# Attention by two key tiles: eight scores in runs of 3, 3 and 2, value products behind each run

## The reference

```python
x = x + 0.5 * ffn(layernorm(x), ...)
x = x + attn(layernorm(x), ...)
x = x + 0.5 * ffn(layernorm(x), ...)

# attn: 16 heads of 16 features; q, k, v and the output are linear with a LoRA update
scores = einsum('bhqd,bhkd->bhqk', q, k) * 16 ** -0.5
out = einsum('bhqk,bhkd->bhqd', softmax(scores), v)
# ffn: silu(x @ gate) * (x @ up) @ down, plus 8 of 512 experts picked by two top-8 of 64 keys
```

## Time and profile before

| what | us |
|---|---|
| median of 3 runs | 845.81 (844.18 to 845.85) |
| the profiled execution: its own time | 844.09 |
| the profiled execution: span, first to last instruction | 842.2 |
| PE busy / DVE busy / ACT busy / POOL busy | 807.8 / 681.3 / 473.4 / 188.5 |
| one attention group, groups 1 to 7 | 20.97 |
| groups 9 to 12, each about | 23.4 |

### The profile page before, as it was taken

The page is one execution under the profiler, slowest core; times in us unless marked ns, Lnnn a source line. Parts: engine busy times, 40 slices in busy tenths (PEclk is TensorE's granted clock), DMA queues, the critical chain, the costliest instruction groups (busy, mean ns, idle before and its releaser), DMA issues.

```text
span 842.2 us, 14291 instructions
## 1 busy us (share of the span) xinstructions
PE 807.8 (96%) x5424; PEld 517.7 (61%) x5424; DVE 681.3 (81%) x1116; ACT 473.4 (56%) x898; POOL 188.5 (22%) x202
## 2 busy tenths in 40 slices
PE   4799999999999999999999999999999999999996
PEld 4687888887876433333333434443458787888885
DVE  5898778787689999999999888889837877976854
ACT  3444333333342788888888888888963343333422
POOL 2441202011111033333332322133430202020200
PEclk9999999999999999999999999999999999999998
DMA  8010000000040242223333222300100000000000
GB/s 274 26 43 10 0 1 1 1 1 1 1 80 9 40 77 53 40 39 64 64 64 63 40 39 39 64 27 26 27 1 1 1 2 26 0 26 1 2 25 26
DMA packets 19300, 27.86 MB, mean 33 GB/s; under 512 B 4576, under 2 KB 13600, under 8 KB 19232
## 3 DMA queue, kind: packets, MB, share of 16 engines
q1 hardware_dynamic: 19040, 26.56, 14.3%
q10 hardware_dynamic: 192, 0.39, 0.2%
HBM read 12.09 MB, written 2.10 MB: 17 GB/s over the span
## 4 chain that ended last, share of the span: by engine, by line
PE 85%; DVE 7%; ACT 4%; issue 2%; DMA 1%; POOL 0%; SPq 0%; DVEq 0%; ACTq 0%
PE front_ps L1608 16%; PE front_ps L1589 13%; PE max_ps L1549 6%; PE ffn_gate_ps L48 5%; PE ffn_out_ps L731 5%; PE ffn_gate_ps L50 5%; PE ffn_gate_ps L49 5%; PE ffn_out_ps L733 5%; PE ffn_out_ps L732 5%; PE ffn_up_ps L50 3%; PE ffn_up_ps L48 3%; PE ffn_up_ps L49 3%; ACT probs L1739 2%; PE ffn_mix_ps L711 2%; DVE norm_xn L139 1%
## 5 line engine op out<-in xcount | busy, mean ns | idle before, releaser
L1819 DVE TENSOR_REDUCE maxima<-max_ps 128x2 f32<-128x1024 f32 x256 | 311.1, 1223 | 29.4 <-PE max_ps L1549 26.9
L1739 ACT ACTIVATE probs<-front_ps 128x512 f32<-128x512 f32 x512 | 277.5, 597 | 39.0 <-PE front_ps L1589 29.3
L847 ACT ACTIVATE ffn_tanh<-ffn_gate_ps 128x512 f32<-128x512 f32 x96 | 57.5, 599 | 222.2 <-PE ffn_gate_ps L50 222.2
L1608 PE MATMUL front_ps<-probs,values 128*32 128x256 f32 x2048 | 163.4, 391 | 4.5 <-ACT mixed_t L1744 4.1
L1080 DVE SCALAR_TENSOR_TENSOR ffn_gated<-ffn_tanh,ffn_gate_ps 128x512 f32<-128x512 f32 x96 | 65.7, 684 | 65.2 <-ACT ffn_tanh L847 65.2
L1608 PEld LDWEIGHTS front_ps<-probs,values 128*32 128x32 f32 x2048 | 40.8, 107 | 95.4 <-issue 55.4
L1589 PE MATMUL front_ps<-q_stack,k_stack 49*128 49x512 f32 x256 | 94.6, 446 | 0.0
L1549 PE MATMUL max_ps<-ffn_xlo,ffn_xhi 48*128 48x512 f32 x256 | 93.7, 447 | 0.0
L1589 PE MATMUL front_ps<-ffn_xhi,ffn_xlo 49*128 49x512 f32 x256 | 91.5, 455 | 0.0
L1489 POOL TENSOR_TENSOR inverse_sum<-turned,minus_one 128x16 f32<-128x16 f32 x15 | 43.7, 2913 | 207.4 <-ACT turned L1751 207.4
L1549 PE MATMUL max_ps<-k_stack,q_stack 48*128 48x512 f32 x256 | 88.0, 455 | 0.6 <-DVE maxima L1819 0.4
(11 more groups left out here) (204 smaller groups left out, 1288.6 us busy)
## 6 DMA issues: line engine op xcount, KB each, us to landing
q_stack<-block SPq DMA_DIRECT2D x48, 64.0 KB, 2.3
ffn_xhi<-block SPq DMA_DIRECT2D x48, 64.0 KB, 2.3
ffn_xlo<-block SPq DMA_DIRECT2D x48, 64.0 KB, 2.3
k_stack<-block SPq DMA_DIRECT2D x42, 64.0 KB, 2.3
x_sb<-in_x SPq DMA_DIRECT2D x4, 512.0 KB, 7.4
out<-x_sb SPq DMA_DIRECT2D x4, 512.0 KB, 2.9
ffn_out_rows<-in_down SPq DMA_DIRECT2D x4, 256.0 KB, 4.8
weights_again<-in_gate SPq DMA_DIRECT2D x2, 512.0 KB, 3.5
```

Source lines behind the costliest of these rows:

```text
L1608: mm = pe.matmul(mixed_ps[strip:strip + STRIP, at:at + HALF // 2], values[g % SLOTS][:, kt, j, :], probs[:, (g * KEY_TILES + kt) % PROBS, ...
L1739: act.activation(probs[:, tile % PROBS, j, half * HALF:(half + 1) * HALF], score_ps[:, n % RING, :], ACT.Exp, scale=SCORE_SCALE).then_inc( ...
L1819: v.reduce_max(maxima[:, g % 2, m // 2, m % 2, :], max_ps[:, m % 2, :, :], axis=AXIS_X).then_inc(pair_max, 1)
```

## The change

- **Two key tiles at a time.** Eight scores and four pairs of two key tiles are put on PE as runs of 3, 3 and 2 scores (`two_key_tiles`). Run A: score, pair, score, score, and only head 1 of the next pair. Then the first half of the mix of the key tile before. Run B: head 0 of that pair, score, score, pair, score; then the second half of that mix. Run C: score, pair, score; then both halves of the mix of the first of the two key tiles. `max_scores` and `ahead` take the heads that they are to do.
- **Single steps.** They stand between run B's mix and run C (`between`, which has the same cases as the loop before): rows at two = 0, `turn_out` at 1, `turn_group_max` at 2, update and product at 3. ACT does six exponentials, then these copies (`copy_mixed` first, at two = 0), then two exponentials. `turn_later` and `rows_later` of group 15 stand before run A, before run B's leading half pair, or behind run B's mix, by a count of runs.
- **Pairs ahead:** 7 in place of 6 (`EARLY`); 5 before the main loop in place of 4. The first two key tiles of group 0 have their own order (`first_two`).
- **Probabilities** have three places in place of two (`PROBS`).
- **Weights again:** the space is halved. The four wide pieces go through the whole of it, one at a time; the late ones still alternate between halves.
- **Used columns:** `copy_turned` and the last group's copy read 17 of each 32 columns (272 in place of 512 elements a row).

```diff
@@ -221,18 +221,15 @@
         self.fetch(sp, dram, piece, self.raw[piece]).then_inc(self.raw_in[piece], 16)
 
     def raw_again(self, i, places):
-        place = places[:, i % 2, :]
-        if self.AGAIN[i].startswith("late"):
-            return place[:, 0:CHUNK]
-        return place.rearrange("p (k f) -> p k f", k=KT)
+        return places[:, i % 2, :] if self.AGAIN[i].startswith("late") else places[:, :, :]
 
     def wait_again(self, pe, piece):
 
         pe.wait_ge(self.again_lo, self.AGAIN.index(piece) + 1)
 
     def load_again(self, sp, dram, i, places):
-        if i >= 2:
-            sp.wait_ge(self.again_lo, i - 1)
+        if i:
+            sp.wait_ge(self.again_lo, i if i <= 4 else max(i - 1, 4))
         self.fetch(sp, dram, self.AGAIN[i], self.raw_again(i, places)).then_inc(self.again_in[i % 2], 16)
 
     def split_again(self, pool, i, places):
...
+STRIP = 32
+
+
+def used_columns(bank):
+
+    return bank.rearrange("p (s x) -> p s x", x=STRIP)[:, :, 0:HD + 1]
+
...
-        act.activation(self.rows.rearrange("p t a b -> p (t a b)"), bank, ACT.Copy).then_inc(self.copied, 1)
+        act.activation(self.rows.rearrange("p t a b -> p (t a) b"), used_columns(bank), ACT.Copy
+                       ).then_inc(self.copied, 1)
...
-    EARLY, EARLY_IN_FRONT = 6, 4
-    RING, PROBS = 3, 2
-    OUT_TURN_AT, MAX_TURN_AT = 2, 6
-    COPY_AFTER = 3
-    UPDATE_AT, TURN_ROWS_AT, PRODUCT_AT = 5, 3, 5
+    EARLY, EARLY_IN_FRONT = 7, 5
+    RING, PROBS = 3, 3
+    TWOS = KEY_TILES // 2
+    TURN_ROWS_AT, OUT_TURN_AT, MAX_TURN_AT, PRODUCT_AT = range(TWOS)
+    UPDATE_AT = PRODUCT_AT
...
-    LATER_TURNS, LATER_ROWS = (1, 2, 3, 4), (3, 4, 5, 6)
+    LATER_TURNS, LATER_ROWS = (2, 3, 5, 6), (5, 6, 8, 9)
...
-        again = sb("weights_again", [P, 2, KT * HALF_INTER], F32)
+        again = sb("weights_again", [P, KT, HALF_INTER], F32)
...
-        turned = sb("turned", [P, 2, KEY_TILES // 2, 4, STRIP], F32)
+        turned = sb("turned", [P, 2, KEY_TILES // 2, 4, HD + 1], F32)
...
-            def max_scores(g, m):
-                if m == 0:
+            def max_scores(g, m, heads=(1, 0)):
+                if g >= GROUPS:
+                    return
+                if m == 0 and 1 in heads:
                     pe.wait_ge(stacks_in[g % SLOTS], (g // SLOTS + 1) * STACK_DMAS * 16)
-                if g * PAIRS + m >= 2:
+                if g * PAIRS + m >= 2 and 1 in heads:
                     pe.wait_ge(pair_max, g * PAIRS + m - 1)
-                max_pair(g, m, 1)
-                max_pair(g, m, 0).then_inc(pair_scored, 1)
+                for j in heads:
+                    scored = max_pair(g, m, j)
+                    if j == 0:
+                        scored.then_inc(pair_scored, 1)
...
-            def ahead(g, step):
+            def ahead(g, step, heads=(1, 0)):
 
                 later, m = divmod(step + EARLY, PAIRS)
-                if g + 1 + later < GROUPS:
-                    max_scores(g + 1 + later, m)
+                max_scores(g + 1 + later, m, heads)
...
+            def first_two():
+
+                early = iter(range(EARLY_IN_FRONT, EARLY + 4))
+                score(0, 0)
+                max_scores(1, next(early))
+                score(0, 1)
+                score(0, 2)
+                max_scores(1, next(early))
+                value_rows(TILES - 2)
+                max_scores(1, next(early))
+                score(0, 3)
+                score(0, 4)
+                max_scores(1, next(early))
+                score(0, 5)
+                value_rows(TILES - 1)
+                max_scores(1, next(early))
+                score(0, 6)
+                max_scores(1, next(early))
+                score(0, 7)
+                mix(0, 0, 0)
+                mix(0, 0, 1)
+
+            def run_later(run):
+
+                if run in LATER_TURNS:
+                    turn_later(LATER_TURNS.index(run))
+                if run in LATER_ROWS:
+                    rows_later(LATER_ROWS.index(run))
+
...
+            def two_key_tiles(g, two):
+                i, step, last_group = 8 * two, 4 * two, g == GROUPS - 1
+                tile = g * KEY_TILES + 2 * two
+                if last_group:
+                    run_later(3 * two)
+                score(g, i)
+                ahead(g, step)
+                score(g, i + 1)
+                score(g, i + 2)
+                ahead(g, step + 1, (1,))
+                mix(*divmod(tile - 1, KEY_TILES), 0)
+                if last_group:
+                    run_later(3 * two + 1)
+                ahead(g, step + 1, (0,))
+                score(g, i + 3)
+                score(g, i + 4)
+                ahead(g, step + 2)
+                score(g, i + 5)
+                mix(*divmod(tile - 1, KEY_TILES), 1)
+                if last_group:
+                    run_later(3 * two + 2)
+                between(g, two)
+                score(g, i + 6)
+                ahead(g, step + 3)
+                score(g, i + 7)
+                mix(g, 2 * two, 0)
+                mix(g, 2 * two, 1)
 
...
-                value_rows(10 + m)
+                if m < 4:
+                    value_rows(10 + m)
+            first_two()
             for g in range(GROUPS):
-                for kt in range(KEY_TILES):
...
-                    score(g, 4 * kt)
-                    ahead(g, 2 * kt)
-                    score(g, 4 * kt + 1)
-                    mix(*divmod(g * KEY_TILES + kt - 1, KEY_TILES), 0)
-                    score(g, 4 * kt + 2)
-                    ahead(g, 2 * kt + 1)
-                    score(g, 4 * kt + 3)
-                    mix(*divmod(g * KEY_TILES + kt - 1, KEY_TILES), 1)
+                for two in range(1 if g == 0 else 0, TWOS):
+                    two_key_tiles(g, two)
...
-                act.activation(turned[:, g % 2, :, :, :].rearrange("p t a b -> p (t a b)"), score_ps[:, n % RING, :],
-                               ACT.Copy).then_inc(ring_out, 1)
+                act.activation(turned[:, g % 2, :, :, :].rearrange("p t a b -> p (t a) b"),
+                               used_columns(score_ps[:, n % RING, :]), ACT.Copy).then_inc(ring_out, 1)
...
-                for kt in range(KEY_TILES):
-                    if kt == OUT_TURN_AT and g:
+                for two in range(TWOS):
+                    for i in range(8 * two, 8 * two + 6):
+                        exponential(g, i)
+                    if two == 0 and g:
+                        copy_mixed(g - 1)
+                    elif two == 0:
+                        value_rows(7)
+                    if two == OUT_TURN_AT and g:
                         copy_turned(g - 1)
-                    if kt == MAX_TURN_AT and g < GROUPS - 1:
+                    if two == MAX_TURN_AT and g < GROUPS - 1:
...
-                    for i in range(4 * kt, 4 * kt + 4):
+                    for i in range(8 * two + 6, 8 * two + 8):
                         exponential(g, i)
-                        if i == COPY_AFTER and g:
-                            copy_mixed(g - 1)
-                        elif i == COPY_AFTER:
-                            value_rows(7)
             copy_mixed(GROUPS - 1)
 
```

62 lines of the change are left out of this document (25 added, 37 removed).

## The result

The changed kernel takes 848.24 us (median of 7 runs, 847.57 to 850.56); the kernel before, run beside it, 844.70 (7 runs, 843.90 to 845.85). The ratio is 1.0047, with a 95% interval of 1.0037 to 1.0057: slower by 3.5 us. The forecast was 847.9 and a change of +2.2. The time came nearer to it than the change did, and that is luck: it was built on a median of 845.81 for the kernel before, which more runs put 1.1 us lower, and this error and the one in the change cancelled. Between the profiled executions the difference is 847.76 - 844.09 = 3.67 us.

A forecast was written before the change was run, and what follows sets the result against it. PE was taken to lead, with DVE close behind. Terms 2.4 - 1.3 + 0.1 + 1.0 + 0 summed to +2.2 us, forecast as 847.9 from the median 845.81; the case's own range was 845.5 to 851, the whole range 838 to 853.

The forecast's parts named there:

- Run B loses 0.32: Run B's mix starts at 2.69 us, not 2.37, held by a reduction; two key tiles take 4.93, not 4.61.
- reduction a: DVE's reduction of run A's whole pair, which frees the bank for run B's whole pair at 2.04 us.
- The price of a change of kind: On PE, fewer switches between scores and mixes cut two key tiles from 4.96 to 4.61 us, 0.35 less.
- The split pair: Pair b's head 1 waits for reduction d, its head 0 follows a mix; two key tiles without a step take 5.1 us.
- DVE's close: DVE's closing of the maxima at two = 2: costs 0.13 us with POOL idle, 0.52 in place of 0.19 with POOL busy.
- Groups without pairs: From the middle of group 14, two key tiles take 0.17 us more than 4.48, six times: +1.0 us.
- The step that failed: In group 0, one pair moves ahead, one change of kind goes, DVE's 16 reductions stay: 0, from -0.7 to +0.7 us.
- The line on stack loads: Single place for weights: stack loads of four groups later wait anyway; nothing to several tenths if a load slips.
- At nothing: Third place of probabilities, narrower copy and single place for weights were put at no gain in the sum.
- the waits of run B are not there: Rival: run B's reduction and exponential waits are absent; -10 us, 836; chance 0.30 together with the rival of all 22 us.
- DVE's cycle is longer: Rival: reductions take 1.22 us instead of 1.14 and POOL is busy at every close; +4.5, 852 us; chance 0.20.
- all of the 22 us arrive: Rival: the whole saving from fewer switches on PE shows, giving 823 us; chance 0.02.

The follow-up runs named there:

- e1: The changed kernel with DVE's reduction of a pair reading only 256 of each head's 512 columns; 845.57 us, ratio 1.0008 to the kernel before.
- e3: The changed kernel with reductions and exponentials both cut to 256 of 512 columns; 830.09 us, ratio 0.9825 to the kernel before.
- e4: The kernel before with reductions and exponentials both cut to 256 of 512 columns; 844.03 us, ratio 0.9999.
- e5: The changed kernel with PE's last two value rows placed before the first score of group 0; 849.50 us, ratio 1.0059 to the kernel before.
- e11: The changed kernel with 6 pairs ahead and 4 before the main loop, as before the change; 848.77 us, ratio 1.0051 to the kernel before.
- e8: The kernel before with only the side edits: third place of probabilities, narrower copies, one place for weights; 844.60 us, ratio 1.0000.
- e2: The changed kernel with each exponential doing only 256 of its 512 columns; 848.41 us, ratio 1.0045 to the kernel before.

## Why the prediction was right, and where its size was wrong

**The bound and the mechanism.** "Run B loses 0.32" was said to come from a reduction first and an exponential right behind it. All three figures for run B's mix, counted from run A's start, were met: 2.69 with both waits (2.70 to 2.72 measured, in all four places of a group), 2.65 with the exponential alone (e1: 2.65), 2.37 with neither (e3: 2.38). The bare length of two key tiles was put at 4.61 and is 4.62 in e3. Counted from run B's own start, the mix comes 1.23 to 1.24 us later at two = 1 and 2 (1.22 was forecast) and 1.09 to 1.12 at two = 3 and 0, where run B itself starts late. The price of a change of kind, 0.35 us for two of them, holds: the twins e3 and e4 differ by 1.39 = 4 x 0.35 in a group. The Trainium skill (TensorEngine Tiling (Array Packing), Key Properties: a change of tiling mode drains TensorE) names that mechanism. The twins agree with it in that fewer changes take less time; that the drain is what is paid, and not another cost of the change, no run separates. The kernel after shows that the rule alone, which would have given about 823 us, says nothing about what the waits leave.

**The split pair.** The order b, c, d, then head 1, and head 0 behind a mix, is what the trace shows, and the 5.1 for two key tiles without slack is 5.09. Three details differ. DVE stands idle twice in two key tiles, not once. Head 1 delays run A's mix by 0.14, not 0.17; and that delay doesn't carry over into run B, whose mix is fixed by reduction a. It is carried by DVE to run C's pair, 0.15 late. The sum comes out the same.

**By terms**, forecast and measured (the lengths are from run A to run A):

| term | forecast | measured |
|---|---|---|
| `two` = 0, 1, 2, 3 | 5.4, 5.5, 5.27, 5.1 | 5.37, 5.54, 5.20, 5.09 |
| groups 1 to 7 and 13, each | +0.3 | +0.20 to +0.24 |
| groups 1 to 7 and 13, together | +2.4 | +1.74 |
| group 8 | +0.1 | -0.07 |
| groups 9 to 12, each | -0.3 | -0.31 |
| groups 9 to 12, together | -1.3 | -1.21 |
| groups 14 and 15 | +1.0 | +0.89 |
| group 0 | 0 (-0.7 to +0.7) | +2.25 |
| sum | +2.2 | +3.6 |

The lengths are from 386.44, 391.81, 397.35, 402.55 and 407.64 in the kernel after. DVE's close was priced at the busy and idle POOL between them and took 0.33 to 0.34 us, so `two` = 2 is 0.07 shorter than I took. Without group 0 the terms came to +1.35 in place of +2.2; the miss in group 0 hid part of that. And 845.81 + 2.2 is 848.0, not 847.9.

**Groups without pairs.** Two key tiles of group 14 (run A, run B, its mix, the next run A):

```profile
601.75 0.73 PE L1602 MATMUL front_ps<-ffn_xhi,ffn_xlo 49*128 49x512 f32 x3
...
603.00 1.47 PE L1602 MATMUL front_ps<-ffn_xhi,ffn_xlo 49*128 49x512 f32 x3
604.39 0.64 PE L1621 MATMUL front_ps<-probs,values 128*32 128x256 f32 x8
...
606.39 0.74 PE L1602 MATMUL front_ps<-ffn_xhi,ffn_xlo 49*128 49x512 f32 x3
```

Run B at +1.25, its mix at +2.64, run C at +3.21, its mixes at +3.64, run A' at +4.64; forecast were 1.24, 2.65, 3.22, 3.65 and 4.65.

**The step that failed** is the last one of the sum: "Group 0: one pair moves ahead of the first score and one change of kind goes, DVE has the same 16 reductions; 0". It counted PE's slots and DVE's reductions and left out two chains that the same edit moves. The value rows end 1.6 us later, SP issues the stack of group 2 behind them, and one more pair ahead needs this stack 1.4 us sooner (the pair is due at 290.45, it was at 291.83). The change took away 3 us of a margin that I had not looked up, and run A lost 1.65 us by it. e5 took away the late load, e11 the early need, and the DMA wait went to nothing and to 0.8. The line on stack loads ("nothing to several tenths if a load slips past a group") looked at loads behind POOL's split in later groups, where none was late: SP's wait for that split grew from 6.8 to 22.5 us, and e8, which has the same single place, is as long as before.

**At nothing.** The narrower copies, the third place and the single place for the weights: e8, ratio 1.0000. The copy of 272 columns takes 0.40 us. The forecast cited 0.53 from the Trainium skill (ScalarE: Activation LUTs, Rules for kernel authors); that line is for a bias given as a pointer operand. Another line of the Trainium skill (the same page, What ACT_TABLE_LOAD costs: 186 ns and 0.833 ns an element with immediate scale and bias) gives an estimate of 0.41, and this agrees with the trace.

**The rivals.** That the waits of run B are not there is refuted: they are, both. That DVE's cycle is longer: three in a row take 3.49 as before, refuted. That all of the 22 us arrive: refuted, though e3 shows that they would, had DVE and ACT been faster.

## What to carry to other kernels

Where three engines are nearly level (here busy for 20.70, 19.59 and 18.45 us of a group of 20.97), a saving on the one that leads is worth only what the rings between them let through: count for each held instruction the slots between it and its releaser in the new order, and price each wait from a row. Two waits that end within 0.05 us of each other hide one another, so that shortening either shows nothing; shorten both in a test before you rule an order out. And when an order is changed, follow its first pass (the front, the first loads) by due times of its own: there the new order lost more than in the seven groups behind it. Last, look at what a test kernel adds: in e2 and e4 the loss behind the constant that POOL wrote was as large as what the shortened instructions brought.
